# Twelve tile statistics on ScalarE, kernel rows by one-hot columns, row edits off VectorE, Toeplitz loads first, decay entries loaded inside the core

## The chip, the core and the metric

The kernel runs on one core of one Trainium2 chip. TensorE multiplies matrices, VectorE and ScalarE work on tiles, GpSimd does small elementwise work, and SyncE issues the transfers. The metric is device time in microseconds: the median of three runs of the kernel before is 955.03 us (954.43 to 955.85).

## The reference

One decoder layer on x (4 sequences of 1024 tokens, width 256) in float32. Its first part, the sequence mixer, is the one that the change touches:

```python
x = x + attn(layernorm(x))     # attn: a second layernorm, then the recurrence below, then @ W_out + b_out, with a residual
dA = exp(-exp(log_A) * dt[:, None]);  dB = B_param * dt[:, None]
h = dA * h + dB * u[..., None]                       # per channel d, 64 states n
y = einsum('dn,bdn->bd', C_param, h) + D_param * u   # for each of the 1024 steps
x = x + xattn(ctx, ctx, layernorm(x))                # 16 heads over 64 keys
x = x + ffn(layernorm(x))                            # silu(w1)*w2, two 1024x1024 gelu layers, w3
```

## The kernel before, in words

All 16 chunks of 64 steps are computed at once. For each of the 256 channels (two sets of 128, in the upper and lower half of the partitions) the recurrence becomes three products: the chunk's own output by a 64x64 lower triangular Toeplitz matrix (`within`, L477), the state that each chunk leaves (`state`, L470, with the entries `EE`, the powers of the decay), and what the carried state adds (`carried`, L484, with `GG`). Between state and carried, VectorE scans over the chunks (L431). The work on 128 channel indices goes in 16 octaves of 8, and the code for it is fully unrolled. Each octave is 48 products.

Before the core (the octaves) the following must be ready.

- `GG` is built by VectorE in six doublings (L337) from its last column. The column sums of `GG`, the kernel rows, are made by TensorE with a block of ones (L461), after D has been added to two of its one-partition rows on VectorE (L397). ScalarE evacuates them (L277), SyncE stores them to HBM (L175) and loads them back with a stride as Toeplitz matrices `ring` (L141), 16 channel indices to a group g, four groups deep. GpSimd masks each (L211). After the kernel rows, VectorE puts the two rows of `GG` back (L411).
- `EE`: SyncE loads each group of 16 with a broadcast (L146), ScalarE takes the exponential (L289).
- The tokens `tok` are normalised: VectorE's bn_stats on all 32 tiles of `xres` (L343, L346), in two batches b of 16, variances (L354), GpSimd's power (L240), spreads (L359, L363), and then 32 instructions for each batch, of which ScalarE takes 20 (`norm_apply`, L284) and VectorE 12 (`norms`, L370). VectorE multiplies by gamma and adds beta (L379, L384), in parts; three betas precede the first octave (`z_b`), the others lie between the scans.

Each engine runs its own queue in order, and semaphores order them against each other. The order is written out by hand. The groups 4 to 7 of the Toeplitz matrices are loaded inside the core, each after an octave that frees its place in the ring (`sync_core`, `w_ps`). In the core ScalarE evacuates each octave's output (L304), takes the later exponentials, and computes the residual base of 32 tiles (L292), to which GpSimd adds a bias (L216).

Of the kernel before, what the change touches and what calls it, by code (L numbers as in the profile page):

```python
# [29 lines left out]
ALU = mybir.AluOpType  # L30
# [24 lines left out]
ACT_SHARE = 20  # L55
# [3 lines left out]
def mixer_parts(nc, ctx, a, t):  # L59
# [7 lines left out]
    def sem(name):  # L67
# [12 lines left out]
    ones = sb("ones", [P, 32], "c")  # L80
# [22 lines left out]
    dtc = sb("dtc", [P, 4], "d")  # L103

    TT = [ring[:, 1024 * k:1024 * (k + 1)] for k in range(4)]
    ksb = ring[:, :].rearrange("p (a m) -> p a m", a=8)
# [7 lines left out]
    kps = [[pair[k][:, 512 * h:512 * (h + 1)] for h in range(2)] for k in (2, 0)]  # L114
# [5 lines left out]
    const, exps, coef, al_st, coef_t, pk_done, g_row, d_add = (  # L120
        sem("m_" + n) for n in ("const", "exps", "coef", "al_st", "coef_t", "pk_done", "g_row", "d_add"))
    k_ps, k_ev, kr_pad, e_rdy, t_mask = (sem("m_" + n) for n in ("k_ps", "k_ev", "kr_pad", "e_rdy", "t_mask"))
    kr_st = sem("m_kr_st")
    T_in = [sem(f"m_T_in{k}") for k in range(4)]
    stat, aggr, sv_rdy, powd, shift, spr, z_rdy, z_dve, z_h, z_b, natural, nat_v = (
# [23 lines left out]
    def sync_mixer(e):  # L149
# [16 lines left out]
        for g in range(2):  # L166
            entries_load(e, g)
        e.dma_start(bo[:, :], a["ab"].partition_broadcast(P)).then_inc(wo_in, 16)
        e.dma_start(woT[:, :, :], a["aW"]).then_inc(wo_in, 16)
        for v in range(4):  # L170
            for h in range(2):
                u = 2 * v + h
                e.wait_ge(k_ev, u + 1)
                c = (1 - h) * (P * L) + v * 2048
                e.dma_start(kr[0, c:c + 2048].rearrange("(q m) -> q m", q=4), ksb[0:P:32, u, :]).then_inc(kr_st, 16)  # L175
        for n in ("xW", "keys", "scl"):
            e.dma_start(t[n], a[n]).then_inc(k_in, 16)
# [4 lines left out]
        for g in range(2, NGRP):  # L182
            entries_load(e, g)
# [34 lines left out]
    def gpsimd_prep(e):  # L218
        e.memset(ident[:, :], 0.0).then_inc(const, 1)
        e.memset(rev[:, :], 0.0).then_inc(const, 1)  # L220
        e.memset(ones[:, :], 1.0).then_inc(const, 1)
# [4 lines left out]
        e.wait_ge(const, 6)  # L226
        e.affine_select(out=ident[:, :], in_=ident[:, :], compare_op=ALU.not_equal, fill=1.0, base=0,
                        pattern=[[-1, P]], channel_multiplier=1).then_inc(const, 1)
        for h in range(2):
            blk = rev[64 * h:64 * h + 64, 64 * h:64 * h + 64]  # L230
            e.wait_ge(const, 7 + h)
# [1258 lines left out]
```

## Time and profile before

| | us |
|---|---|
| median of three runs | 955.03 |
| the profiled execution | 954.79 |
| its span | 953.0 |
| TensorE busy | 877.2 (92%) |
| VectorE busy | 519.0 (54%) |
| ScalarE busy | 495.5 (52%) |
| GpSimd busy | 182.4 (19%) |

The span is the time from the first to the last instruction of one profiled execution. PE is TensorE, DVE is VectorE, ACT is ScalarE, POOL is GpSimd, SP is SyncE and SPq its queue of transfers. A "releaser" is what ended an engine's idle time. PEclk is the granted clock of TensorE as a share of full speed, and a DMA share of 1.00 means that all 16 engines of the core moved data all the time. In the slices of the page (one fortieth of the span, 23.8 us, each) TensorE's busy tenths begin 1, 0, 7, 9: it is nearly idle up to 48 us. The core of the mixer ends at about 102 us, the cross-attention of the first block at 155, and the loop over the other blocks fills the rest.

### The profile page before, as it was taken

What the parts mean: (1) busy time and instruction counts of PE and PEld (TensorE: products, weight loads), DVE (VectorE), ACT (ScalarE), POOL (GpSimd) and SP (SyncE); (2) the same over time, 40 slices, a digit from 0 to 9 for tenths busy, and PEclk for the clock granted to TensorE, in tenths of its full rate; (3) what the DMA queues carried; (4) which work ended last, traced back from release to release, by engine and by line L of the source; (5) the groups of instructions that cost most, each with busy time, mean ns of one, the idle gap of its engine ahead of it and who ended that gap; (6) DMA issues with size and microseconds to landing.
All of it is one profiled execution on the core that took longest, in us unless ns stands there. A gap on an engine that the chain in (4) does not pass through costs nothing.

```text
span 953.0 us, 15162 instructions
## 1 busy us (share of the span) xinstructions
PE 877.2 (92%) x5570; PEld 697.1 (73%) x5570; DVE 519.0 (54%) x927; ACT 495.5 (52%) x761; POOL 182.4 (19%) x201
## 2 busy tenths in 40 slices
PE   1079898999999999999999999999999999999996
PEld 0078876777777777777777777778778877777885
DVE  7996485555456454555555555554556465544411
ACT  2836542476356735663475536653675356636331
POOL 1567600500040003200230014000500050003000
PEclk9679999899999999999999999999999999999999
DMA  9971798500110001000200020001000110001000
GB/s 340 224 170 49 269 413 303 214 1 1 51 44 0 0 23 71 0 0 22 72 0 0 0 94 0 0 0 72 22 0 0 50 44 0 0 22 44 1 1 24
DMA packets 15784, 62.82 MB, mean 66 GB/s; under 512 B 2867, under 2 KB 4534, under 8 KB 14934
## 3 DMA queue, kind: packets, MB, share of 16 engines
q1 hardware_dynamic: 15718, 62.35, 19.2%
q8 instruction: 23, 0.38, 0.2%
q14 instruction: 11, 0.09, 0.0%
q0 software_dynamic: 32, 0.00, 0.0%
HBM read 50.16 MB, written 23.72 MB: 78 GB/s over the span
## 4 chain that ended last, share of the span: by engine, by line
PE 77%; DVE 11%; ACT 5%; issue 4%; DMA 1%; DVEq 0%; ACTq 0%; SPq 0%
PE pair L1182 47%; PE pair L1169 10%; PE pair L1118 3%; PE pair L1107 3%; PE pair L1134 3%; PE pair L539 2%; PE pair L470 2%; PE pair L1127 2%; PE pair L477 1%; PE pair L1074 1%; DVE red L932 1%; PE pair L484 1%; DVE vbuf L997 1%; DVE st L868 1%; DVE GG L337 1%
## 5 line engine op out<-in xcount | busy, mean ns | idle before, releaser
L803 ACT ACTIVATE vbuf<-pair,scl 128x512 f32<-128x512 f32 x128 | 87.8, 686 | 237.1 <-PE pair L1182 231.3
L1182 PE MATMUL pair<-h1hi,h_turned 128*128 128x512 f32 x512 | 204.0, 398 | 1.6 <-DVE h1lo L968 1.6
L1182 PE MATMUL pair<-h2hi,h_turned 128*128 128x512 f32 x512 | 202.6, 396 | 0.0
L1182 PE MATMUL pair<-h1lo,h_turned 128*128 128x512 f32 x512 | 199.8, 390 | 0.0
L1182 PE MATMUL pair<-h2lo,h_turned 128*128 128x512 f32 x512 | 199.6, 390 | 0.0
L968 DVE TENSOR_TENSOR h1lo<-vbuf,h1hi 128x512 fp32r<-128x512 f32 x80 | 57.7, 721 | 118.5 <-ACT h1hi L804 117.7
L1182 PEld LDWEIGHTS pair<-h1hi,h_turned 128*128 128x128 f32 x512 | 96.1, 188 | 34.3 <-issue 10.5
L1182 PEld LDWEIGHTS pair<-h2hi,h_turned 128*128 128x128 f32 x512 | 96.1, 188 | 25.2 <-issue 5.9
L968 DVE TENSOR_TENSOR h2lo<-vbuf,h2hi 128x512 fp32r<-128x512 f32 x64 | 44.2, 690 | 123.5 <-ACT h2hi L804 123.5
L1182 PEld LDWEIGHTS pair<-h2lo,h_turned 128*128 128x128 f32 x512 | 96.2, 188 | 19.3
L1182 PEld LDWEIGHTS pair<-h1lo,h_turned 128*128 128x128 f32 x512 | 96.2, 188 | 18.9
L1169 PE MATMUL pair<-zThi,w_turned 128*128 128x512 f32 x224 | 92.3, 412 | 5.5 <-DVE vbuf L997 5.4
L1169 PE MATMUL pair<-zTlo,w_turned 128*128 128x512 f32 x224 | 89.0, 398 | 0.0
L697 POOL TENSOR_TENSOR lnv<-lnv 128x4 f32<-128x4 f32 x16 | 16.3, 1016 | 374.6 <-DVE lnv L875 350.8
L997 DVE SCALAR_TENSOR_TENSOR vbuf<-pair,scl,sg 128x512 f32<-128x512 f32 x64 | 47.9, 749 | 66.7 <-ACT sg L792 51.2
L756 ACT ACT_TABLE_LOAD x65 | 83.4, 1283 | 1.2
L792 ACT ACTIVATE sg<-pair,scl 128x512 f32<-128x512 f32 x64 | 44.1, 689 | 65.3 <-PE pair L1169 55.0
L729 POOL TENSOR_TENSOR h1lo<-vbuf,h1hi 128x512 fp32r<-128x512 f32 x48 | 62.0, 1292 | 57.9 <-ACT h1hi L795 57.9
L470 PE MATMUL pair<-tok,EE 64*64 64x60 f32 x512 | 39.1, 278 | 24.5 <-DVE tok L384 23.2
L1169 PEld LDWEIGHTS pair<-zThi,w_turned 128*128 128x128 f32 x224 | 43.0, 192 | 22.0 <-DVE vbuf L997 11.3
L711 POOL TENSOR_TENSOR kblk<-keys,hmask 128x256 f32<-128x256 f32 x18 | 10.7, 613 | 214.7 <-PE pair L1107 214.7
L1182 PE MATMUL pair<-h1hi,w_turned 128*128 128x512 f32 x128 | 50.4, 394 | 0.0
(138 smaller groups left out, 1455.0 us busy)
## 6 DMA issues: line engine op xcount, KB each, us to landing
h_turned<-d_h SPq DMA_DIRECT2D x2, 4096.0 KB, 16.0
xres<-in_x SPq DMA_DIRECT2D x8, 512.0 KB, 7.3
tok<-in_xs SPq DMA_DIRECT2D x8, 512.0 KB, 12.2
EE<-alpha_rows SPq DMA_DIRECT2D x16, 256.0 KB, 11.6
ring<-kernel_rows SPq DMA_DIRECT2D x16, 256.0 KB, 4.4
x_rows<-x1t SPq DMA_DIRECT2D x8, 512.0 KB, 2.6
xr<-x_rows SPq DMA_DIRECT2D x8, 512.0 KB, 3.5
out<-xr SPq DMA_DIRECT2D x16, 256.0 KB, 2.1
```

What stands on the lines that cost most here:

```text
L470: ins = e.matmul(out, EE[L * h:L * h + L, i, :], rhs, start=True, stop=True)
L729: e.tensor_tensor(h1[1][:, m, :], vb[:, m % 2, :], h1[0][:, m, :], ALU.subtract).then_inc(S["lo"], 1)
L756: e.activation(warm[:, 1:2], warm[:, 0:1], function).then_inc(S["warm"], 1)
L792: e.activation(sg[:, m % 2, :], pair[m % 2][:, 0:512], ACT.Silu, scale=sc1[:, m:m + 1]).then_inc(S["sg_rdy"], 1)
L803: e.activation(vb[:, s % 2, :], h_ps[s % 4], ACT.Gelu, scale=sc)
L968: e.tensor_tensor(dst[1][:, n % HC, :], vb[:, n % 2, :], dst[0][:, n % HC, :], ALU.subtract).then_inc(S["lo"], 1)
L997: e.scalar_tensor_tensor(vb[:, m % 2, :], pair[m % 2][:, 512:1024], sc2[:, m:m + 1], sg[:, m % 2, :], ALU.mult, ALU.mult).then_inc(S["v_rd ...
L1107: ins = e.matmul(pair[2][:, g * BLK + b * 256:g * BLK + (b + 1) * 256], qa[64 * g:64 * g + 64, h, tile * P:(tile + 1) * P], kblk[64 * g:64 ...
L1118: ins = e.transpose(pair[3][:, b * BLK + r * P:b * BLK + (r + 1) * P], unit(j, u)[:, r // 2, c:c + P], ident[:, :])
L1134: ins = e.matmul(pair[3][:, m * DM:(m + 1) * DM], qa[:, k, m * P:(m + 1) * P], xwoT[:, k, :], start=(k == 0), stop=(k == DH - 1))
L1169: ins = e.matmul(pair[m % 2][:, 512 * g:512 * g + 512], w[:, k, m * P:(m + 1) * P], zT[part][:, k * BLK:(k + 1) * BLK], start=(k == 0 and ...
L1182: ins = e.matmul(bank, w[:, k, m * P:(m + 1) * P], src[part][:, k, :], start=(k == 0 and part == 0), stop=(k == HC - 1 and part == 1))
```

## The change

Five things are changed.

1. Tiles 4 to 15 of the first batch get their mean and variance on ScalarE (`tile_stats`): a Copy with an accumulated sum, two small scalings, and a Square with an accumulated sum. The elementwise outputs go to a scrap region of PSUM. VectorE keeps tiles 0 to 3 and 16 to 31. ScalarE's share of a batch's normalisations falls from 20 to 18.
2. The kernel rows are accumulated over the four groups v into one pair of banks, each group with a window of `pick` in which one column is one, so that two evacuations take the place of eight, and eight stores read four strided partitions each. ScalarE evacuates after six normalisations.
3. The copy, the addition and the restoring of the two rows of `GG` go to ScalarE and GpSimd. The clearing of two PSUM banks and of the first column of `dec` goes to the start of VectorE's program.
4. SyncE stores the kernel rows first, loads one group of entries, then the Toeplitz groups 0 to 3 alternating with entries 1 to 3, then the weights. Entries 4 to 7 are loaded inside the core, each behind the Toeplitz group of its number.
5. TensorE does three products of 512 columns into a free bank when two betas are done. VectorE does gamma and beta twice before its normalisations of the second batch. The second batch's exponentials and the residual bases come later on ScalarE, GpSimd's power over 32 columns comes behind the four masks.

```diff
-ACT_SHARE = 20
+ACT_SHARE = 18
+ACT_STATS = (4, 16)
...
-    kps = [[pair[k][:, 512 * h:512 * (h + 1)] for h in range(2)] for k in (2, 0)]
+    kps = [pair[2][:, 512 * h:512 * (h + 1)] for h in range(2)]
+    junk = [pair[0][:, DM * k:DM * (k + 1)] for k in range(4)]
...
 def sync_mixer(e):
...
+        for h in range(2):
+            e.wait_ge(k_ev, h + 1)
+            for r in range(4):
+                c = (1 - h) * (P * L) + 2048 * r
+                e.dma_start(kr[0, c:c + 2048].rearrange("(q m) -> q m", q=4), ksb[r:P:32, h, :]).then_inc(kr_st, 16)
         e.wait_ge(al_st, 32)
...
+        entries_load(e, 0)
         e.wait_ge(kr_st, 128)
         e.wait_ge(kr_pad, 16)
         for g in range(4):
             tt_load(e, g)
-        for g in range(2, NGRP):
-            entries_load(e, g)
+            if g > 0:
+                entries_load(e, g)
...
 def sync_core(e):
         for g in range(4, NGRP):
             e.wait_ge(w_ps, 2 * (g - 4) + 2)
             tt_load(e, g)
+            entries_load(e, g)
...
 def gpsimd_prep(e):
+        e.wait_ge(d_in, 32)
+        e.wait_ge(g_row, 7)
+        e.wait_ge(w_row, 2)
+        for row in (0, N):
+            v = GG[row:row + 1, :, L - 1]
+            e.tensor_tensor(v, v, edit[row:row + 1, 0, :], ALU.add).then_inc(d_add, 1)
+        e.wait_ge(d_add, 2)
+        power(0)
+        e.wait_ge(k_ps, 1)
+        e.wait_ge(powd, 1)
+        for row in (0, N):
+            e.tensor_copy(GG[row:row + 1, :, L - 1], edit[row:row + 1, 1, :]).then_inc(g_back, 1)
+        e.wait_ge(g_back, 2)
+        power(1)
+        for g in range(4):
+            mask(e, g)
...
 def scalar(e):
+        def tile_stats(first, until):
+            here, n = slice(first, until), until - ACT_STATS[0]
+            e.wait_ge(xr_in[first // 4], 16)
+            if n > 4:
+                e.wait_ge(t_var, n - 4)
+            for j in range(first, until):
+                e.activation(junk[j % 4], xres[:, j, :], ACT.Copy, accum_out=tsum[:, 0, j:j + 1]).then_inc(t_sum, 1)
+            e.wait_ge(t_sum, n)
+            e.activation(tsum[:, 1, here], tsum[:, 0, here], ACT.Copy, scale=-1.0 / (16 * DM)).then_inc(t_mean, 1)
+            e.activation(mvn[:, here, 0], tsum[:, 0, here], ACT.Copy, scale=1.0 / DM).then_inc(t_mean, 1)
+            e.wait_ge(t_mean, n // 2)
+            for j in range(first, until):
+                e.activation(junk[j % 4], xres[:, j, :], ACT.Square, bias=tsum[:, 1, j:j + 1], scale=1.0 / 16, accum_out=mvn[:, j, 1:2]).then_inc(t_var, 1)
...
+                if c == 6:
+                    row_evac()
...
 def vector(e):
-        stats(0, 4)
-        double(4)
-        stats(4, 8)
-        double(5)
...
-        stats(8, 16)
-        variances(0)
-        stats(16, 26)
+        stats(0, ACT_STATS[0])
+        last_two(0)
+        for k in range(4, 6):
+            double(k)
+        stats(SB, SB + 4)
+        variances(0)
+        stats(SB + 4, SB + 12)
         spreads(0)
-        stats(26, 32)
+        stats(SB + 12, TILES)
...
 def tensor(e):
-                    ins = e.matmul(kps[v % 2][h][32 * q:32 * q + 32, :], ones[N * h:N * h + N, 0:32], ..., start=True, stop=True)
+                    ins = e.matmul(kps[h][32 * q:32 * q + 32, :], pick[N * h:N * h + N, 3 - v:35 - v], ..., start=(v == 0), stop=(v == 3))
...
+        e.wait_ge(z_b, 2)
+        for _ in range(3):
+            e.matmul(pair[3][:, 0:BLK], ident[:, :], GGf[:, 0:BLK], start=True, stop=True)
```

SyncE's transfers ahead of the core, before (`alpha_rows` are the decay entries in HBM, `kernel_rows` the stored kernel rows; m_al_st and m_k_ev wait for the entries' store and for the evacuations):

```order
L146 DMA EE<-alpha_rows 64x1024 [waits m_al_st]
L146 DMA EE<-alpha_rows 64x1024 x3
L168 DMA bo<-in_ab 128x256
L169 DMA woT<-in_aW 128x512
L175 DMA kernel_rows<-ring 4x512 [waits m_k_ev] x8
L177 DMA xW<-in_xW 128x512
L177 DMA keys<-in_keys 128x512
L177 DMA scl<-in_scl 128x34
L141 DMA ring<-kernel_rows 64x1024 [waits m_kr_pad,m_kr_st]
L141 DMA ring<-kernel_rows 64x1024 x7
L146 DMA EE<-alpha_rows 64x1024 x12
```

And now:

```order
L173 DMA kernel_rows<-ring 4x512 x3
L150 DMA EE<-alpha_rows 64x1024 [waits m_al_st]
L150 DMA EE<-alpha_rows 64x1024
L145 DMA ring<-kernel_rows 64x1024 [waits m_kr_pad,m_kr_st]
L145 DMA ring<-kernel_rows 64x1024 x3
L150 DMA EE<-alpha_rows 64x1024 x2
L145 DMA ring<-kernel_rows 64x1024 x2
L150 DMA EE<-alpha_rows 64x1024 x2
L145 DMA ring<-kernel_rows 64x1024 x2
L150 DMA EE<-alpha_rows 64x1024 x2
L182 DMA bo<-in_ab 128x256
```

The two loads of entries (`EE`) with the Toeplitz loads (`ring`) alternate, the stores stand first, and only the groups 0 to 3 of both are left here.

SyncE's transfers inside the core, before (the last row is the first load of the feed-forward weights):

```order
L141 DMA ring<-kernel_rows 64x1024 [waits m_w_ps]
L141 DMA ring<-kernel_rows 64x1024
L141 DMA ring<-kernel_rows 64x1024 [waits m_w_ps]
L141 DMA ring<-kernel_rows 64x1024
L141 DMA ring<-kernel_rows 64x1024 [waits m_w_ps]
```

And now, the first two of four such groups:

```order
L145 DMA ring<-kernel_rows 64x1024 [waits m_w_ps]
L145 DMA ring<-kernel_rows 64x1024
L150 DMA EE<-alpha_rows 64x1024 x2
L145 DMA ring<-kernel_rows 64x1024 [waits m_w_ps]
L145 DMA ring<-kernel_rows 64x1024
L150 DMA EE<-alpha_rows 64x1024 x2
```

Behind each pair of Toeplitz loads stands a pair of loads of entries.

VectorE from the second batch's spreads on, before (`gam` and `bet` are gamma and beta, `spread` holds scale and shift):

```order
L363 COPY spread<-rn 64x2x16 [waits m_shift]
L363 COPY spread<-rn 64x2x16 x3
L411 COPY GG<-edit 1x128 [waits m_k_ps]
L411 COPY GG<-edit 1x128
L412 MEMSET dec 128x128
L379 TENSOR_TENSOR tok<-tok,gam 128x32x32 [waits m_z_dve,m_z_rdy,m_bc_in]
L370 TENSOR_SCALAR tok<-tok,spread 128x128 [waits m_x_in6,m_spr]
L370 TENSOR_SCALAR tok<-tok,spread 128x128 x3
L370 TENSOR_SCALAR tok<-tok,spread 128x128 [waits m_x_in7]
L370 TENSOR_SCALAR tok<-tok,spread 128x128 x7
L384 TENSOR_TENSOR tok<-tok,bet 128x32x32 [waits m_z_h]
L379 TENSOR_TENSOR tok<-tok,gam 128x32x32 [waits m_z_dve,m_z_rdy]
```

And now:

```order
L408 COPY spread<-rn 64x2x16 [waits m_shift]
L408 COPY spread<-rn 64x2x16 x3
L424 TENSOR_TENSOR tok<-tok,gam 128x32x32 [waits m_z_dve,m_z_rdy,m_bc_in]
L429 TENSOR_TENSOR tok<-tok,bet 128x32x32 [waits m_z_h]
L424 TENSOR_TENSOR tok<-tok,gam 128x32x32 [waits m_z_dve,m_z_rdy]
L429 TENSOR_TENSOR tok<-tok,bet 128x32x32 [waits m_z_h]
L415 TENSOR_SCALAR tok<-tok,spread 128x128 [waits m_x_in6,m_spr]
L415 TENSOR_SCALAR tok<-tok,spread 128x128 x5
L415 TENSOR_SCALAR tok<-tok,spread 128x128 [waits m_x_in7]
L415 TENSOR_SCALAR tok<-tok,spread 128x128 x7
L424 TENSOR_TENSOR tok<-tok,gam 128x32x32 [waits m_z_dve,m_z_rdy]
L429 TENSOR_TENSOR tok<-tok,bet 128x32x32 [waits m_z_h]
```

The two copies into `GG` and the clearing of `dec` are gone; two gammas and two betas now precede the 14 normalisations of the second batch, where one gamma preceded 12.

## Rows read from the trace of the kernel before

**Rows 1.** Chain of waits up to 84 us: start, length, what.
```profile
28.66 3.63 ACT tok L284 x10
...
37.47 1.23 DVE tok L379
...
49.53 1.86 PE pair L470 x30
...
55.20 3.20 issue
...
70.45 1.61 issue
...
83.41 1.27 issue
```

**Rows 2.** DMA view, instruction queue, windows 55.4:56, 69:70 and 84:98: packets, MB, share.
```profile
q8 instruction: 1, 0.02, 13.5%
...
q8 instruction: 1, 0.02, 6.9%
...
q8 instruction: 4, 0.07, 1.9%
```

**Rows 3.** Time line of SyncE from 64 to 70 us: start, length, what.
```profile
65.67 1.09 SPq L141 DMA_DIRECT2D ring<-kernel_rows  x2
```

**Rows 4.** Windows view: length, each engine busy (instructions), PEclk, DMA share, GB/s.
```profile
52.00:54.00 2.00, 2.00 (x80) 2.00 (x74) 2.00 (x5) 0.00 (x0) 1.80 (x3) 0.50 1.04 229
64.00:66.00 2.00, 2.00 (x84) 2.00 (x78) 2.00 (x4) 0.05 (x1) 1.31 (x2) 1.00 0.04 8
66.50:69.50 3.00, 2.90 (x110) 2.80 (x107) 3.00 (x8) 2.67 (x6) 1.36 (x1) 1.00 0.71 175
```

**Rows 5.** Time line of VectorE: start, length, instruction, idle time before it.
```profile
6.04 0.58 DVE L332 COPY edit<-pair 1x128 f32<-1x128 f32 x2
...
14.87 4.40 DVE L337 TENSOR_TENSOR GG<-GG,pk 128x4096 f32<-128x4096 f32 x1
19.40 0.84 DVE L397 TENSOR_TENSOR GG<-GG,edit 1x128 f32<-1x128 f32 x2
...
26.81 0.40 DVE L343 BATCH_NORM_STATS2 stn<-xres 128x6 f32<-128x256 f32 x1
...
27.20 0.40 DVE L343 BATCH_NORM_STATS2 stn<-xres 128x6 f32<-128x256 f32 x1
...
27.77 0.80 DVE L363 COPY spread<-rn 64x32 f32<-64x32 f32 x4
```

**Rows 6.** Time line of GpSimd, power and first mask.
```profile
23.96 2.93 POOL L240 TENSOR_TENSOR rn<-sv,mhalf 128x16 f32<-128x16 f32 x1 [20.06 <-DVE sv L354]
...
40.30 2.42 POOL L211 TENSOR_SCALAR_AFFINE_SELECT ring<-ring 64x1024 f32<-64x1024 f32 x2 [5.90 <-DMA ring<-kernel_rows]
```

**Rows 7.** Time line of ScalarE.
```profile
3.47 0.20 ACT L264 ACTIVATE dtc<-dtc 128x2 f32<-128x2 f32 x1 [1.37 <-DMA dtc<-in_log_dt]
...
5.99 0.95 ACT L269 ACTIVATE pk<-pair 128x128 f32<-128x128 f32 x5
...
22.44 1.08 ACT L277 ACTIVATE ring<-pair 128x512 f32<-128x512 f32 x2 [13.50 <-PE pair L461]
...
28.66 7.81 ACT L284 ACTIVATE tok<-tok,spread 128x128 f32<-128x128 f32 x20 [1.09 <-issue]
...
67.49 1.08 ACT L292 ACTIVATE xres<-xres,ngn,rsn 128x256 f32<-128x256 f32 x2
```

**Rows 8.** Windows view, VectorE on tile tok alone: length, busy (instructions), PEclk, DMA.
```profile
32.50:35.50 3.00, 2.96 (x12) 0.50 0.43 144
...
40.00:42.00 2.00, 2.00 (x4) 0.50 1.04 236
```

**Rows 9.** Time line of SyncE, first Toeplitz loads.
```profile
35.45 4.96 SPq L141 DMA_DIRECT2D ring<-kernel_rows  x8
```

**Rows 10.** Chain of waits at 199 us, 512-column products.
```profile
198.90 3.66 PE pair L1182 x16
```

More of the change, by code:

```diff
@@ L79, in mixer_parts @@
     rev = sb("rev", [P, P], "c")
-    ones = sb("ones", [P, 32], "c")
+    pick = sb("pick", [P, 35], "c")
     stn = sb("stn", [P, TILES, 6], "d")
@@ L220, in gpsimd_prep @@
         e.memset(rev[:, :], 0.0).then_inc(const, 1)
-        e.memset(ones[:, :], 1.0).then_inc(const, 1)
+        e.memset(pick[:, :], 0.0).then_inc(const, 1)
         e.memset(mhalf[:, :], -0.5).then_inc(const, 1)
@@ L230, in gpsimd_prep, with power @@
             blk = rev[64 * h:64 * h + 64, 64 * h:64 * h + 64]
-            e.wait_ge(const, 7 + h)
+            e.wait_ge(const, 8 + h)
             e.affine_select(out=blk, in_=blk, compare_op=ALU.not_equal, fill=1.0, base=-63,
                             pattern=[[1, 64]], channel_multiplier=1).then_inc(const, 1)
-        e.wait_ge(const, 9)
+        e.wait_ge(const, 10)
         e.dma_start(kr[:, DM * L:DM * L + L], rev[0:1, L:2 * L]).then_inc(kr_pad, 16)
-        for b in range(2):
+        def power(b):
             here = slice(SB * b, SB * b + SB)
@@ L245, in gpsimd_prep @@
         e.wait_ge(natural, 1)
-        for g in range(1, 4):
-            mask(e, g)
-        e.wait_ge(t_mask, 8)
     def gpsimd_core(e):
@@ L292, in residual_base @@
             e.activation(xres[:, j, :], xres[:, j, :], ACT.Identity, bias=ngn[:, j:j + 1], scale=rsn[:, j:j + 1]).then_inc(base, 1)
-        for v in range(4):
-            row_evac(v)
-        e.wait_ge(const, 9)
+        for first in range(*ACT_STATS, 4):
+            tile_stats(first, first + 4)
+        e.wait_ge(const, 10)
         norm_apply(0)
-        entry_exp(0)
         norm_apply(1)
-        for g in range(1, 3):
+        for g in range(3):
             entry_exp(g)
@@ L304, in scalar @@
             e.activation(tok[:, :, OCT * o:OCT * o + OCT], yps[o % 4].rearrange("p (i c) -> p c i", i=OCT), ACT.Copy).then_inc(y_out, 1)
-            if o % 2 == 0 and 3 + o // 2 < NGRP:
+            if o % 2 == 1 and 3 + o // 2 < NGRP:
                 entry_exp(3 + o // 2)
-            if o == 2:
+            if o == 5:
                 e.wait_ge(natural, 3)
-            until = 0 if o < 2 else min(2 * o - 2 + max(0, o - 8), TILES)
+            until = 0 if o < 5 else min(3 * (o - 4), TILES)
             for j in range(done, until):
@@ L321, in vector @@
     def vector(e):
+        for k in range(2):
+            e.memset(hps[k], 0.0).then_inc(h_zero, 1)
+        e.memset(dec[:, :, 0], 0.0).then_inc(dec0, 1)
         e.wait_ge(exps, 2)
@@ L330, in vector @@
         e.tensor_copy(GG[:, :, L - 1:L], wT.unsqueeze(2)).then_inc(g_row, 1)
-        for row in (0, N):
-            e.tensor_copy(edit[row:row + 1, 1, :], wT[row:row + 1, :]).then_inc(d_add, 1)
         def double(k):
@@ L343, in stats, with last_two @@
                 e.bn_stats(stn[:, j, :], xres[:, j, :]).then_inc(stat, 1)
+                n = j if j < SB else j - (ACT_STATS[1] - ACT_STATS[0])
                 if j % SB >= 2:
-                    e.wait_ge(stat, j - 1)
+                    e.wait_ge(stat, n - 1)
                     e.bn_aggr(mvn[:, j - 2, :], stn[:, j - 2, :]).then_inc(aggr, 1)
+        def last_two(b):
+            until, n = (ACT_STATS[0], TILES)[b], ACT_STATS[0] + SB * b
+            for j in (until - 2, until - 1):
+                e.wait_ge(stat, n - (until - 1 - j))
+                e.bn_aggr(mvn[:, j, :], stn[:, j, :]).then_inc(aggr, 1)
         def variances(b):
-            for j in (SB * b + SB - 2, SB * b + SB - 1):
-                e.wait_ge(stat, j + 1)
-                e.bn_aggr(mvn[:, j, :], stn[:, j, :]).then_inc(aggr, 1)
-            e.wait_ge(aggr, SB * b + SB)
+            n = ACT_STATS[0] + SB * b
+            if b == 0:
+                e.wait_ge(t_var, ACT_STATS[1] - ACT_STATS[0])
+            e.wait_ge(aggr, n)
             here = slice(SB * b, SB * b + SB)
@@ L418, in vector @@
         beta(1)
+        norms(1)
         gamma(2)
```

68 lines of the change are left out of this document (27 added, 41 removed).

## The prediction

> **What bounds the kernel now.** I read the busy table and the slices first: over the 953.0 us TensorE is busy 92%, and the slices in which it is not are the first three, about 70 us. The change ends before the cross-attention, so I read only the stretch up to 105 us, in the chain of waits. The reader sees there [rows 1]: ScalarE's twenty normalisations (20 instructions from 28.66, two pieces of ten), a gamma product at 37.47, then VectorE's own normalisations with more gamma and beta, and TensorE's first state product at 49.53. Behind it the chain has three stretches called issue: 3.20 us at 55.20, 1.61 at 70.45, 1.27 at 83.41. No engine is waited for in them. What ends them is seen only in the DMA view: a queue named instruction brings single packets of 0.02 MB, and one lies at 55.4 to 56, one at 69 to 70 [rows 2], each some 2.5 to 3 us before TensorE goes on. From 84 to 98, with nothing else to load, four come in 14 us [rows 2], one each 3.5 us. So TensorE's unrolled code is streamed, and it runs little ahead. A packet that is late is lost time. At 65.67 two Toeplitz loads are issued [rows 3]; the DMA engines are 71% busy from 66.5 to 69.5 [rows 4], the packet comes behind them, and TensorE stands 1.61 us.
>
> The clock reads 0.50 from 52 to 54 and 1.00 from 64 to 66 (1.2 and 2.4 GHz), but these small products pass at 80 and 84 per 2 us [rows 4]: 5%.
>
> **The change, part by part.**
>
> *Up to the first spreads.* Gone from VectorE before the doublings: two row copies (0.58 us at 6.04 [rows 5]); with an overlap of 0.2 the doublings begin 0.4 earlier. The last doubling (4.40 us, [rows 5]) now stands behind 4 statistics instead of 8. A statistic with its aggregation costs 0.39 (two starts are 26.81 and 27.20 [rows 5]), so the last doubling ends at about 19.3 - 0.4 - 4 x 0.39 = 17.3 us. The two row edits (0.84 [rows 5]) go to GpSimd; one-partition adds on GpSimd aren't in the trace, I take 1.0 (between nothing and the 2.93 of its 16-element power [rows 6]). The kernel rows start at 18.5 instead of 20.4, which buys nothing: they are evacuated only after six normalisations on ScalarE.
>
> ScalarE's statistics begin when the decay broadcast and two row copies are done, about 9.4. One pass over 128x256 with no pointer lies between the 128x128 copies (five in 0.95, 0.17 apart) and the 128x512 ones (two in 1.08): 0.31. With two pointers it is 0.49 apart (two in 1.08), with one, like the squares, I take 0.40 [rows 7]. A group of four tiles is 4 x 0.31 + 4 x 0.40 + two tiny scalings and three waits on its own results, together 0.75: 3.6 us. The accumulator output isn't in the trace. At least it is free; as a tiny instruction of its own (0.20 us [rows 7], 0.11 apart) it adds 8 x 0.11 = 0.9; at 0.3 each it adds 2.4. I take 0.9, so three groups take 13.5 us and end at 22.9 (20.2 to 27.4).
>
> VectorE waits for it: it has only four more statistics in front (to 18.9). Power on GpSimd 2.93 [rows 6], with eight statistics beside it, then one shift and four copies (0.80 [rows 5]), 1.0: the first spreads are ready at about 27.1, against 28.6 (27.77 + 0.80 [rows 5]). Call this moment A. It is 1.5 us earlier (24.4 to 31.6 by the two ends). Twelve statistics off VectorE would be 4.7 us; most of it becomes a wait for ScalarE.
>
> *From A to the core.* ScalarE: 18 normalisations at 0.39 (twenty take 7.81 [rows 7]) and the two evacuations (1.08) are 8.1, before 7.8. VectorE then does gamma, beta, gamma, beta (1.14 to 1.25 each, after [rows 1]), 4.8: A + 13.0. Only now its 14 normalisations. Alone each takes 0.24 (12 in 2.96 us); while GpSimd masks, four in 2.00 [rows 8]. The masks start when the first Toeplitz load lands. The evacuated rows are ready at A + 3.0 to A + 3.5. Eight stores follow, 0.5 us each (two issues take 1.09 [rows 3]), then some 2 us until the last has landed (my estimate for 8 KB on quiet engines). The first Toeplitz load is issued at A + 8.9 (before at 35.45 [rows 9], which was A + 6.9). From issue to mask it took 4.85 us before (40.30 [rows 6]); the mask starts at A + 13.7, before at A + 11.7. So masks 0 and 1 (2.42 us a pair [rows 6]) lie on the normalisations: four of the 14 at 1.2, ten at 0.24, 7.2 us. With gamma and beta 2.4 more the core starts at A + 22.6 = 49.7, against 49.53. If the masks missed them it were 3.8 earlier. ScalarE's first decay exponential is ready at A + 16.4, the first mask at A + 16.2: hidden. The three dummy matmuls sit in A + 13 to A + 22.6; by the 0.23 us in which a 512-column pass runs at the full clock (16 in 3.66 [rows 10]), 3 x 4 passes at half of it are 5.5 us, hidden too. They give the first products the full clock perhaps; by the 5% above that is 0.3 us.
>
> *Code and loads.* The first packet is asked for shortly into the core. Before, it came between 55.4 and 56 [rows 2], behind full engines (busy share 1.04 at 52 to 54 [rows 4]), and TensorE went on at 58.40 [rows 1]. Now 1.5 MB of entries less (three groups behind the first, not six) stand in the queue together with the Toeplitz rows (at 229 GB/s [rows 4] 14 load instructions of 0.26 MB are 16 us from A + 10): they end at about A + 26 = 53, and 1.1 MB of weights and biases at 56. A packet asked for at 50.5 then passes when the entries are through, at 53.7, and TensorE goes on 2.7 later, at 56.4: 2.0 us earlier than 58.40. The packet after it is no longer held by that queue, for which I take 0.4 more: 2.4 earlier.
>
> But groups 4 to 7 of the entries now go out behind the Toeplitz loads inside the core: four instructions and 1 MB each time instead of 0.5. The engines are full for about 5 us instead of 2.7 (from 66.5 on at 175 GB/s over 3 us [rows 4]). Code packets come every 3.5 us and these loads every two octaves, about 5.4 us: a window of 2.7 catches some (two clear stalls, 1.61 and 1.27 [rows 1]; I allow 0.4 for smaller ones), a window of 5 catches nearly all. Counting on from the restart with one packet each 3.5 us and a load pair each two octaves, four of seven packets fall into a window, each held back 1.6 (as at 70.45) to 2.1 us (a load that lasts longer): 4 x 1.8 = 7.3, against 3.3. That is +4.0. SyncE's queue has nothing urgent behind these loads. Group 4's exponential is needed only three octaves on: hidden.
>
> Sum on the profiled execution: -2.4 + 4.0 = +1.6 on 953.0. Behind the core nothing changes: ScalarE still has three residual tiles in front of its last two evacuations; its two last tiles come behind them, in the time in which TensorE turns the first block. GpSimd's 32-element power moves behind the four masks and is wanted by VectorE at octave 4, some 5 us after it is ready. The profiled run took 954.79, 1.79 over its span and 0.24 under the median of 955.03; I add the 1.6 to the median: **956.6 us**.
>
> **The rivals.** *The code is not held back (952.6).* If a packet gets in between the loads, the +4.0 vanishes and -2.4 stays. For it: four Toeplitz pairs are loaded inside the core, and only two of them show a stretch of over 1 us. Against it: the stalls at 70.45 and 83.41 stand exactly where loads and packet met, with only 0.5 MB loaded. The Trainium skill, "Runtime: NRT & Kernel Launch", section "Instruction fetch mechanics", says that the sequencer fetches the next page while it executes the current one, and that the cost of a boundary is mostly hidden. By that rule this rival would be the forecast. The trace disagrees in this stage, with 3.20, 1.61 and 1.27 us.
>
> *ScalarE's statistics are dear (959.6).* The point is the wait of the first variances for the last of the twelve. If an accumulating pass costs 0.3 more, it ends at 27.4 and A at 31.6, 3.0 later than before; the core starts 4.5 later than I put it, part of which the emptier queue gives back, so I price it at +3 over my sum. It decides from the point at which a group of four takes more than 5.0 us (then A is where it was). For it: VectorE has nothing to do but wait from 18.9. Against it: the nearest rows are cheap.
>
> *The start is early (954).* The accumulator is free and A at 24.4, or the masks miss the normalisations. The start gains 3 us, but the first packet is held longer in a fuller queue, and the +4.0 stays: about -1 in all.
>
> **Chances.** Forecast 45%, code not held 25%, dear statistics 20%, early start 10%. The forecast's own range is 954.5 to 958.5 (windows that catch three or five packets, 1.8 us each). To hold 8 in 10 it must take in most of both rivals: 952 to 960. A measurement of this kernel tells 0.2%, 1.9 us. Faster by more: most of the second case and a little of the last, 24%. Slower by more: the dear case and two fifths of the forecast, 36%. Within: 40%.
>
> **What would show it.** Right: VectorE idle several us before its first variances, the spreads near 27, the first state product near 50, the first issue stretch ended near 56.4, and then about four stretches of issue over 1 us from 60 to 87 us, each with a code packet at the end of a Toeplitz and entries load. Wrong: issue stretches that are gone or no longer than before (then the first rival), or ScalarE's twelve statistics past 25 us (the second). What would make the total wrong with every step right is the phase: how the packets fall against the loads is a matter of some tenths of a us.

## The result

| | before | after |
|---|---|---|
| median, us | 954.58 (951.36 to 955.85, 6 runs) | 958.36 (956.86 to 961.93, 6 runs) |
| profiled execution, us | 954.79 | 958.09 |
| its span | 953.0 | 956.4 |
| TensorE busy | 877.2 | 880.7 |

The ratio is 1.0051, interval [1.0026, 1.0075]: slower by more than the 0.2% that can be told from no change. The forecast was 956.6, and its range of 952 to 960 holds the time. TensorE's busy time grows by 3.5 us, but that isn't the cause: the three dummy products alone take 4.4 us (from 40.4 to 44.9), and TensorE waits anyway until 51.

The profile after. The chain of waits (start, length, what), which answers to [rows 1]:

```profile
22.49 4.81 issue
27.30 2.42 ACT tok L321 x6
...
40.18 7.45 DVE tok L415 x14
...
48.98 2.05 DVE tok L429
...
51.07 1.86 PE pair L507 x30
...
56.21 2.38 issue
...
66.36 1.34 issue
...
71.31 2.28 issue
...
81.55 1.41 issue
...
86.59 1.70 issue
```

L415 is VectorE's fourteen normalisations of the second batch, L429 its beta, L507 the first state product. Four issue stretches of 1.34 to 2.28 us follow the first one, where before had two (1.61 and 1.27). The DMA view has one packet of the instruction queue in each of 65 to 66, 70.5 to 71.5, 80 to 81 and 85 to 86 us; TensorE goes on at 67.7, 73.6, 83.0 and 88.3, each time 2.4 to 2.9 us behind its packet. SyncE begins to issue the four groups of loads at 59.7, 65.5, 74.8 and 80.8, 4.7 to 5.6 us ahead of these packets.

Time line of ScalarE, a part of the first group of four statistics, and the end of the last (to [rows 7]):

```profile
10.67 0.37 ACT L301 ACTIVATE pair<-xres 128x256 f32<-128x256 f32 x1
10.97 0.19 ACT L301 ACTIVATION_READ_ACCUMULATOR pair<-xres 128x1 f32 x1
11.07 0.36 ACT L301 ACTIVATE pair<-xres 128x256 f32<-128x256 f32 x1
...
12.93 0.46 ACT L307 ACTIVATE pair<-xres,tsum 128x256 f32<-128x256 f32 x1
13.32 0.19 ACT L307 ACTIVATION_READ_ACCUMULATOR pair<-xres,tsum 128x1 f32 x1
13.42 0.46 ACT L307 ACTIVATE pair<-xres,tsum 128x256 f32<-128x256 f32 x1
...
22.30 0.19 ACT L307 ACTIVATION_READ_ACCUMULATOR pair<-xres,tsum 128x1 f32 x1
```

An accumulated sum is a second instruction of 0.19 us. Passes follow each other every 0.40 (sums) and 0.49 us (squares).

Time line of VectorE and then of GpSimd (to [rows 5, 6, 8]); brackets hold the idle time before:

```profile
22.52 0.18 DVE L399 TENSOR_SCALAR sv<-mvn 128x16 f32<-128x16 f32 x1 [3.36 <-ACT pair L307]
...
26.02 1.20 DVE L408 COPY spread<-rn 64x32 f32<-64x32 f32 x4
...
29.27 3.67 DVE L415 TENSOR_SCALAR tok<-tok,spread 128x128 f32<-128x128 f32 x14
...
40.18 7.43 DVE L415 TENSOR_SCALAR tok<-tok,spread 128x128 f32<-128x128 f32 x14
```

```profile
17.86 1.14 POOL L251 TENSOR_TENSOR GG<-GG,edit 1x128 f32<-1x128 f32 x2 [13.80 <-DVE GG L375]
...
41.47 5.05 POOL L214 TENSOR_SCALAR_AFFINE_SELECT ring<-ring 64x1024 f32<-64x1024 f32 x4 [9.10 <-DMA ring<-kernel_rows]
```

The same number of normalisations, fourteen, take 3.67 us at 29.27 and 7.43 at 40.18, when GpSimd's masks run beside them. The time line taken instruction by instruction shows how: beside the four masks (5.05 us, 1.26 each) four of the fourteen take 1.24 to 1.31 us each, the others about 0.26. This is the 4 x 1.2 and 10 x 0.24 of the prediction.

Time line of SyncE (to [rows 3, 9]), and the DMA view's instruction queue from 55.8 to 56.4 us (to [rows 2]):

```profile
35.74 2.44 SPq L145 DMA_DIRECT2D ring<-kernel_rows  x4
...
65.50 1.22 SPq L145 DMA_DIRECT2D ring<-kernel_rows  x2
66.76 1.24 SPq L150 DMA_DIRECT2D EE<-alpha_rows  x2
```

```profile
q8 instruction: 1, 0.02, 11.3%
```

The windows view, columns as in [rows 4]. First 48 to 56 us of after:

```profile
48.00:52.00 4.00, 0.93 (x18) 0.93 (x20) 3.96 (x3) 1.15 (x1) 3.63 (x2) 0.50 1.03 228
52.00:54.00 2.00, 2.00 (x66) 2.00 (x66) 2.00 (x4) 0.00 (x0) 1.16 (x2) 0.52 1.02 221
54.00:56.00 2.00, 2.00 (x79) 1.98 (x74) 2.00 (x3) 0.00 (x0) 1.85 (x3) 1.00 1.06 340
```

The first packet comes at 56.0 to 56.1. The DMA engines are full until then and for 1 us longer. From 54 on they move 340 GB/s instead of 221: the entries are through, and what moves are the weights and biases.

Then the measure for the rest of this document: the window from the restart behind the first code packet over some 765 products of the core. Its length less TensorE's busy time is what TensorE lost there. Before, and under it after:

```profile
58.40:84.70 26.30, 23.00 (x767) 21.90 (x767) 21.12 (x41) 14.81 (x24) 14.41 (x19) 0.94 0.41 102
```

```profile
58.60:88.30 29.70, 22.62 (x765) 21.77 (x766) 20.57 (x42) 13.05 (x21) 18.97 (x21) 0.94 0.56 145
```

Before loses 3.30 us there, after 7.08. That is +3.8. The window is 3.4 us longer (TensorE is busy 0.4 less in it), and so is the span: nearly the whole result lies in these 30 us.

### The profile page after: what moved, and what is told of

It reads as the page before. It is cut to its first block, busy times and chain, and to the rows that moved or that the text cites. A ratio compares the mean times of both kernels' runs of the same rounds, so it can differ in the third digit from the quotient of the medians.

```text
span 956.4 us, 15206 instructions
## 1 busy us (share of the span) xinstructions
PE 880.7 (92%) x5576; PEld 698.2 (73%) x5576; DVE 515.4 (54%) x901; ACT 503.4 (53%) x807; POOL 184.0 (19%) x206
## 4 chain that ended last, share of the span: by engine, by line
PE 77%; DVE 9%; ACT 5%; issue 5%; DMA 1%; DVEq 0%; ACTq 0%; SPq 0%
PE pair L1219 47%; PE pair L1206 10%; PE pair L1155 3%; PE pair L1144 3%; PE pair L1171 3%; PE pair L507 2%; PE pair L576 2%; PE pair L1164 2%; PE pair L1111 1%; PE pair L514 1%; DVE red L969 1%; PE pair L521 1%; DVE vbuf L1034 1%; DVE st L905 1%; DVE red L984 1%
## 5 line engine op out<-in xcount | busy, mean ns | idle before, releaser
L1219 PE MATMUL pair<-h1hi,w_turned 128*128 128x512 f32 x128 | 50.4, 394 | 0.0
L507 PE MATMUL pair<-tok,EE 64*64 64x60 f32 x512 | 39.6, 277 | 11.4 <-DVE tok L429 6.2
```

The source lines that it names most:

```text
L507: ins = e.matmul(out, EE[L * h:L * h + L, i, :], rhs, start=True, stop=True)
L1219: ins = e.matmul(bank, w[:, k, m * P:(m + 1) * P], src[part][:, k, :], start=(k == 0 and part == 0), stop=(k == HC - 1 and part == 1))
```

## The experiments

Ratios are to the kernel before, run beside each on the same chip, five rounds each. The theory: TensorE's code comes in packets, one for each 256 matmul and weight-load instructions; a packet that is asked for while data fill the DMA engines is late, and TensorE stands for it. Times within a kernel are of one profiled execution each, and the ratios of the timed runs decide.

**e1: before, with idle bytes.** Two entry loads that nothing uses behind each of the four Toeplitz pairs in the core.

```diff
+            for h in range(2):
+                e.dma_start(EE[L * h:L * h + L, GRP * (g - 4):GRP * (g - 3), :].rearrange("p d n -> p (d n)"),
+                            bass.AP(t["alS_h"], (8 * h + g - 4) * (GRP * N), [[0, L], [1, GRP * N]])).then_inc(again, 16)
```

> The kernel before, with one thing added: inside the core each Toeplitz pair (groups 4 to 7) is followed by two loads of 0.26 MB that read the raw decay entries of a group already used once more into its own place, which nobody reads. Theory (code packets of TensorE stand behind data on the DMA engines): four load windows of about 5 us instead of 2.7, so issue stretches grow by 3 to 4 us in all between 60 and 88 us and the median rises by 3.5 us (ratio about 1.0037), with the same start of the core (49.5) and the same first restart (58.4). Rival (the changed kernel is late because ScalarE's exponentials or GpSimd's masks come late and hold the products): nobody waits for these loads, so nothing changes (ratio 1.000).

Measured: 958.62, ratio 1.0043 [1.0028, 1.0058]. The windows view, the same products:

```profile
59.90:88.70 28.80, 22.16 (x767) 21.05 (x766) 20.15 (x39) 14.79 (x24) 14.29 (x13) 1.00 0.56 150
```

6.64 us are lost, 3.3 more than before. No instruction of the core waits for these bytes, so as many bytes as the change adds bring nearly its whole loss (3.3 of 3.8) without a late exponential or mask. One part of the expectation missed: with nothing changed ahead of the core, its first product starts at 51.3 here and not at 49.5, and TensorE goes on at 59.9 and not at 58.4.

**e2: before, with entries 4 to 7 in the core** as the change has them.

```diff
-        for g in range(2, NGRP):
+        for g in range(2, 4):
             entries_load(e, g)
...
             tt_load(e, g)
+            entries_load(e, g)
```

> The kernel before, with the entries of groups 4 to 7 loaded inside the core, each behind its Toeplitz pair, and nothing else changed. Theory: the core starts at 49.5 as before, the queue ahead of it is 1 MB x 2 shorter (about 9 us of loads) and is through at about 51, so the first issue stretch ends near 55 instead of 58.4 (-3.4); the four windows in the core then cost +3.5. Sum about 0 (ratio 0.998 to 1.002). Rival (only the loads inside the core matter, the first stretch has another cause than the queue): first stretch stays, ratio 1.0037.

Measured: 953.70, ratio 0.9997 [0.9985, 1.0008]. The core starts at 50.4, and the queue runs empty as it does (DMA share 0.61 from 50 to 51, 0.00 from 51 to 52). The first packet (instruction queue, 51.8 to 52.4 us) comes 1.7 us behind the start, where before it was 5.9; the windows view follows:

```profile
q8 instruction: 1, 0.02, 9.6%
```

```profile
52.00:54.00 2.00, 2.00 (x76) 2.00 (x76) 1.97 (x6) 0.00 (x0) 1.93 (x2) 0.50 0.03 8
55.80:82.10 26.30, 22.12 (x773) 21.14 (x766) 23.79 (x46) 14.85 (x24) 16.53 (x21) 0.99 0.63 164
```

TensorE passes the first page at 55.8 without a stop, where before did at 58.4. The same loads inside the core cost 4.18 us here, 0.9 more than before, not the 3.3 of e1. In this execution the gain that the prediction put on the start exists, with an empty queue, and the price of the loads depends on how they fall. But it is the fastest of the kernel's twelve runs (951.01, the median is 953.70), and the timed ratio shows no gain in the sum.

**e3: the changed kernel, with entries 4 to 7 ahead of the core** (behind the Toeplitz groups; the edit of e2 turned round).

```diff
+        for g in range(4, NGRP):
+            entries_load(e, g)
...
             tt_load(e, g)
-            entries_load(e, g)
```

> The changed kernel with the entries of groups 4 to 7 ahead of the core again, behind the other loads of entries and ahead of the weights. Theory: the four long issue stretches between 60 and 88 us go back to two of 1 to 2 us, but the queue is full until about 62, so the first restart is near 59.3 and the second packet is held too; +1.5 us against the kernel before, 2 us faster than the changed kernel (ratio 1.0015). Rival (the later start of the core is the whole loss): still 1.005.

Measured: 959.22, ratio 1.0053 [1.0040, 1.0067]: missed. The chain shows why:

```profile
55.41 3.23 issue
...
63.04 3.71 issue
```

The first stretch is 3.23 us and the second, 3.71, is new. The 2 MB moved ahead keep the engines full beyond 64 (DMA share 1.06 from 62 to 64), and the second packet is late too; it lies at 64 to 65. Of the stretches behind it three of 1.01, 0.74 and 1.45 us are left. The loss has moved towards the start of the core.

**e4: the changed kernel, with all statistics on VectorE.**

```diff
-        for first in range(*ACT_STATS, 4):
-            tile_stats(first, first + 4)
...
-        stats(0, ACT_STATS[0])
+        stats(0, 4)
...
+        stats(4, 16)
+        last_two(0)
```

> The changed kernel with all 32 statistics on VectorE again (ScalarE's share of the normalisations stays 18). Theory: VectorE's idle 3.4 us before the first variances vanish and the variances come at the same 22.5 us; the first spreads come 1.3 us later because twelve and not eight statistics lie behind the power; the total is 1 us above the changed kernel (ratio against before about 1.0062). Rival (ScalarE's statistics are what costs): faster than the changed kernel by 1 us or more.

Measured: 959.80, ratio 1.0048 [1.0035, 1.0061], against 1.0051 of the changed kernel: neither the 1 us more that was expected nor the rival's 1 us less. VectorE's time line has the spreads 0.85 us later:

```profile
27.27 0.80 DVE L404 COPY spread<-rn 64x32 f32<-64x32 f32 x4
```

Yet the first state product starts at 50.9 against 51.07: VectorE's last beta takes 1.22 us here and 2.04 beside a mask in the changed kernel, the normalisations 7.25 and 7.43, and this takes the 0.85 back. The twelve statistics on ScalarE neither gain nor cost anything that can be measured.

**e5: the changed kernel, with the second batch's normalisations directly behind their spreads,** before gamma and beta and so before the masks.

```diff
+        norms(1)
...
-        norms(1)
```

> The changed kernel with VectorE's 14 normalisations of the second batch directly behind the second spreads (33.9 us), ahead of gamma and beta and of the masks. Theory: alone they take 3.4 us instead of 7.4 and fill the 1.5 us in which VectorE waited for ScalarE, so the core starts near 45 to 46 instead of 51.1; but the queue is full then, the first packet is held for the full 4.5 us and the second until the weights are through (56), so only about 4 us reach the end: ratio against before about 1.001 (after: 1.0051). Rival (the start of the core decides alone): 5.5 us or more, ratio 0.999 or less. Rival (the code queue decides alone and the start nothing): ratio stays 1.005.

Measured: 955.75, ratio 1.0009 [1.0000, 1.0018]. VectorE's time line, and the chain:

```profile
33.77 3.68 DVE L415 TENSOR_SCALAR tok<-tok,spread 128x128 f32<-128x128 f32 x14
```

```profile
47.17 1.70 PE pair L507 x30
...
52.15 2.76 issue
```

3.68 in place of 7.43, the core starts 3.9 earlier and goes on at 54.9 instead of 58.6. This is worth 0.4%, as was expected. The 3.9 us are not the masks' effect alone: the 1.52 us in which VectorE waited are filled too, some gammas and betas now lie beside masks instead (2.17 and 2.05 us at 42.15 and 44.35), and at the end the core waits for the dummy products until 47.1.

One more thing is seen here. SyncE issues the same loads at the same times as in the changed kernel (to 0.2 us), and the entries are through at the same time (the rate rises in 54 to 55 in both). The first packet comes at 52.2, in the middle of the entries, and not at 56.0. It lies 5.1 us behind the core's start, in the changed kernel 5.0. So the packet goes with TensorE's program there, not with the end of the entries or of the weights.

**e6: e5, with entries 0 to 3 loaded ahead of the stores of the kernel rows,** when the queue is idle.

```diff
+        e.wait_ge(al_st, 32)
+        for g in range(4):
+            entries_load(e, g)
         for h in range(2):
             e.wait_ge(k_ev, h + 1)
...
-        e.wait_ge(al_st, 32)
-        entries_load(e, 0)
...
-            if g > 0:
-                entries_load(e, g)
```

> The kernel of e5 with the entries of groups 0 to 3 moved ahead of the stores of the kernel rows, into the time from about 24 to 34 us in which the DMA engines of the changed kernel are idle; groups 4 to 7 stay inside the core. Theory: Toeplitz loads and weights are through by about 49, the first packet is held 3 us at most, the second not at all; the first restart is near 52 (after: 58.6), the four long stretches in the core stay. Ratio against before about 0.9965. Rival (the queue ahead of the core doesn't matter once the start is early): same as e5.

Measured: 953.38, ratio 0.9981 [0.9972, 0.9991], a gain of 0.3% on e5 where 0.45% was expected. TensorE passes the first packet without a stretch of over 0.3 us, but loses 6.4 in the rest.

**e7: e6, with entries 0 to 5 early, 6 and 7 behind the Toeplitz groups, none in the core.**

```diff
-        for g in range(4):
+        for g in range(6):
...
+        for g in range(6, NGRP):
+            entries_load(e, g)
...
-            entries_load(e, g)
```

> The kernel of e6 with groups 0 to 5 ahead of the stores and 6 and 7 behind the Toeplitz loads, none inside the core. Theory: two stalls of 1 to 2 us remain in the core instead of four, which gives back about 3.5 us, but the queue is full until 56 again and holds the first two packets (restart near 54.6, second boundary near 59), which costs about the same: ratio 0.9965, between 0.995 and 0.999. Rival (only the loads inside the core cost): 3.5 us faster than e6.

Measured: 953.76, ratio 0.9985 [0.9975, 0.9994], inside its range but no better than e6. The chain:

```profile
55.47 3.95 issue
...
63.96 1.77 issue
...
81.72 1.45 issue
```

The first packet lies at 48.3, only 1.6 us behind the start of the core at 46.7, with the engines full, and TensorE doesn't stand for it; for the second, at 56.7 with the engines as full, it stood 3.95 us. How long a full queue holds a packet isn't settled by its being full.

**e8: e6, without the three products of 512 columns ahead of the core.**

```diff
-        e.wait_ge(pk_done, 7)
-        e.wait_ge(w_row, 2)
-        e.wait_ge(z_b, 2)
-        for _ in range(3):
-            e.matmul(pair[3][:, 0:BLK], ident[:, :], GGf[:, 0:BLK], start=True, stop=True)
```

> The kernel of e6 without the three products of 512 columns that TensorE does into a free bank before the core. Theory: the small products pass at nearly the same pace at either clock and the first blocks of code wait for their packets anyway: within 0.5 us of e6, and the clock reads 0.50 in the first products instead of 1.00. Rival (the warming is worth its place): 1 us or more slower than e6.

Measured: 952.88, ratio 0.9977 [0.9968, 0.9986], as e6. TensorE's time line of e6 has the dummy products in its way; that of e8 starts the core 2.2 us earlier:

```profile
42.38 5.42 PE L498 MATMUL pair<-GG,ident 128*128 128x512 f32 x6 [17.38 <-DVE tok L428]
47.73 1.76 PE L506 MATMUL pair<-tok,EE 64*64 64x60 f32 x30
```

```profile
45.55 1.86 PE L501 MATMUL pair<-tok,EE 64*64 64x60 f32 x30 [20.65 <-DVE tok L428]
```

The packets lie at 50.5 (e6) and 50.7 (e8), and TensorE goes on behind both at 53.1: the packet bounds it there, and not the start of the core. Why the two packets lie together, 2.8 and 5.1 us behind their starts, isn't shown; the engines are full at that time in both. And the clock (0.50 in e8 from 46 to 50, 1.00 in e6 from 48 to 52) decides nothing here.

**e9: before, with the Toeplitz pairs issued at chosen products.** SyncE waits for TensorE to pass a fixed product, chosen just behind the point where a packet has been asked for.

```diff
-        for g in range(4, NGRP):
-            e.wait_ge(w_ps, 2 * (g - 4) + 2)
-            tt_load(e, g)
+        for n, (toeplitz, entries) in enumerate((((4,), ()), ((5,), ()), ((6,), ()), ((7,), ()))):
+            e.wait_ge(pace, n + 1)
+            for g in toeplitz:
+                tt_load(e, g)
...
+                    if (o, c) in ((3, 0), (4, 3), (7, 0), (8, 3)):
+                        ins.then_inc(pace, 1)
```

> The kernel before, with one edit: the four Toeplitz pairs of groups 4 to 7 are not issued as soon as their buffer is free, but when TensorE reaches a fixed product of the core, chosen to fall just behind the point at which a code packet has been asked for (one every 256 recorded instructions). Nothing is computed differently. Theory (a code packet that stands behind data in the queues is held, and the hold is lost 1:1): the two issue stretches of rows 1 at 70.45 (1.61) and 83.41 (1.27) go, 2.5 to 3 us less, ratio 0.997. Rival (bytes brought in during the core decide, whenever they are asked for): no change, ratio 1.000. Rival with the other sign (the Toeplitz pairs now arrive late): a wait for the load at the first product of a group, 1 us and more, ratio above 1.001.

Measured: 953.21, ratio 0.9983 [0.9974, 0.9992].

```profile
58.80:81.80 23.00, 22.66 (x766) 21.77 (x765) 19.49 (x42) 14.80 (x24) 8.98 (x12) 0.93 0.33 97
```

The window loses 0.34 us in place of 3.30. The same four pairs are loaded, and no wait for them comes up in it. Timed, the gain is 1.6 us, not the 2.5 to 3 expected. Behind this window 256 instructions take 3.9 to 4.1 us (before 3.6) with the DMA engines idle (share 0.02): from 85.7 to 97.7 TensorE is busy for 10.94 of 12.00 us, standing 0.3 to 0.4 at the end of each page. That gives a part of the 3.0 back; why it does is open.

**e10: the changed kernel, with all eight loads in the core so placed.** Order: entries 4, Toeplitz 4, 5, entries 5, Toeplitz 6, then Toeplitz 7 with entries 6, then entries 7.

```diff
+        for n, (toeplitz, entries) in enumerate((((), (4,)), ((4,), ()), ((5,), ()), ((), (5,)), ((6,), ()), ((7,), (6,)), ((), (7,)))):
+            e.wait_ge(pace, n + 1)
...
+                    if (o, c) in ((1, 5), (3, 0), (4, 3), (5, 5), (7, 0), (8, 3), (9, 5)):
+                        ins.then_inc(pace, 1)
```

> The changed kernel, with one edit: the four Toeplitz pairs and four entry loads inside the core are issued one or two at a time when TensorE reaches fixed products, each just behind the point at which a code packet has been asked for. Theory of held packets: of the four long issue stretches of the changed kernel inside the core (1.34, 2.28, 1.41, 1.70) at most one stays (two loads share one point), 5 us less than the changed kernel, ratio to before 1.000 (0.998 to 1.002). Rival (the bytes inside the core decide, not their moment): ratio stays 1.005.

Measured: 953.75, ratio 0.9984 [0.9971, 0.9997], 0.7% under the changed kernel and inside its range of 0.998 to 1.002. Windows, then the chain behind it:

```profile
58.20:81.00 22.80, 22.39 (x768) 21.71 (x770) 19.96 (x42) 10.73 (x17) 12.50 (x15) 0.93 0.45 134
```

```profile
80.59 6.45 DMA EE<-alpha_rows
```

0.41 us lost in place of 7.08. The core starts no earlier than in the changed kernel (the restart is at 58.2, there at 58.6). The entries issued last, now late, become a wait of their own: between 84.7 and 88.3 TensorE stands for some 3 us, and a part of the gain is left there.

**e11: e8, so paced, with entries 6 early too.**

```diff
-        for g in range(4):
+        for g in (0, 1, 2, 3, 6):
             entries_load(e, g)
```

> The kernel of e8 with the paced loads of e10, and the entries of group 6 ahead of the core as well, so that no point carries two loads. Theory of held packets: three of e8's four stretches in the core go, 4 to 6 us less than e8 (952.88), ratio to before 0.992 to 0.994. Rival (moment does not matter): as e8, 0.998.

Measured: 947.57, ratio 0.9914 [0.9901, 0.9928], a little under the 0.992 to 0.994 expected; e8 had 0.9977. It beats both kernels, the one before by 0.9%.

```profile
53.10:76.00 22.90, 21.34 (x761) 20.74 (x762) 20.30 (x42) 11.40 (x18) 19.21 (x17) 1.00 0.48 134
```

1.56 us are lost there; e8 loses 6.34 over the same products.

**e12: e9 at the wrong moment,** 1.75 us later, and nothing else changed.

```diff
-                    if (o, c) in ((3, 0), (4, 3), (7, 0), (8, 3)):
+                    if (o, c) in ((3, 5), (5, 0), (7, 5), (9, 0)):
```

> The kernel of e9, in which the same four Toeplitz pairs are issued at four other products, 1.75 us later, so that a pair is on its way when the next code packet is asked for. Number, size and spacing of the loads are those of e9, and each group still lands 11 us and more before its first product. Theory (the hold of a code packet behind data decides): each of four packets starts 1 to 2 us later than in e9, four issue stretches of about 1 to 1.5 us come back, 3 to 5 us more than e9 (953.21), ratio to before 1.001 to 1.004. Rival (it is the spacing of the loads that helped in e9, not their moment): as e9, 0.998.

Measured: 955.80, ratio 0.9991 [0.9982, 1.0000].

```profile
59.60:84.20 24.60, 22.44 (x764) 21.61 (x763) 19.51 (x39) 14.77 (x24) 8.00 (x8) 0.93 0.27 71
```

2.16 us lost against 0.34 in e9: the direction is that of the theory, the size about half of what was expected. The expected ratio of 1.001 to 1.004 was missed. In time the difference to e9 is 0.08%, and the two intervals overlap, so by the timed runs alone moment and spacing aren't told apart.

## Why the prediction was right or wrong

*Up to the first spreads: right.* ScalarE's statistics were put to end at 22.9; they end at 22.49. A was put at 27.1; the spreads are out at 27.22. The accumulator read is the 0.1 us apart that the prediction took. The two row edits on GpSimd cost 1.14 for 1.0.

*From A to the core: right in its kind, 1.4 us short.* VectorE begins the fourteen normalisations at 40.18 (put at A + 13.0 = 40.1, with the wait for ScalarE's eighteen in it), the mask is at 41.47 (put at 40.8), the normalisations take 7.4 (7.2), and the core starts at 51.07 (49.7). Up to here it is right to some tenths; what was missed is a last beta of 2.04 us beside a mask, put at 1.2, and some tenths around it. The same happens by chance in the kernel before: e1, e9 and e12 have its program ahead of the core unchanged, and their first products start at 51.30, 50.23 and 51.26, against 49.53 in its own profile. VectorE's last gamma or beta beside a mask, 2.04 to 2.16 us instead of 1.2, is the difference. So the 1.4 us are no more than executions of one program differ by. The dummy products (L499, 4.44 us from 40.41) are hidden, as forecast.

In e5 the fourteen normalisations without masks take 3.75 us less, near the 3.8 of the prediction.

*The start gain of 2.4: wrong.* This is the term that failed. The packet was to pass at 53.7, when the entries are through, and TensorE to go on at 56.4. The packet lies at 56.0, 2 us into the weights, and TensorE goes on at 58.6, 0.2 later than in the profile before. The 2.5 us from packet to restart are near the forecast (2.7). What failed is the step that ties the packet to the end of the entries. The entries are through at about 54 (put at 53), and the packet doesn't come with them; in e5, with the same queue, it comes before that, at 52.2. In both it lies 5.0 to 5.1 us behind the core's start, before 5.9, and 1.7 in e2 with the queue empty. So an emptier but still full queue brought 0.9 us in these two profiles, and the later start of the core took them. By the other executions the gain is no larger: with the start of the kernel before TensorE goes on at 58.4, 59.9, 58.8 and 59.6 (before, e1, e9, e12), with that of the changed kernel at 58.6 and 58.2 (after, e10), 0.8 earlier in the mean. What sets the packet's time in a full queue stays open: e7 has it 1.6 us behind the core's start.

*Code and loads, +4.0: right.* 7.3 against 3.3 was forecast for the stalls behind the restart (its 4 x 1.8 is 7.2); 7.08 against 3.30 is what the two windows lose. Four stretches of over 1 us stand there, each with a packet, as forecast. That the sizes agree so well is in part luck: the prediction itself calls the phase of packets and loads a matter of tenths, and e2, with the same loads in the core, loses 4.18. e1 shows the same with bytes that no one uses, e9 and e10 that nearly all of it goes (0.34 and 0.41 left) with the same loads issued at other moments. The rule beside which the prediction set a rival, the Trainium skill's "Runtime: NRT & Kernel Launch", "Instruction fetch mechanics" (the next page is fetched during the current one, the boundary is mostly hidden), agrees with e9's window, where the loads are out of the way and the loss is 0.34 us over six packets. It doesn't agree with the windows before and after, nor quite with e9 behind its window (1.06 us in 12.00, engines idle).

*Why the hold varies: open.* In e7 the first packet is hardly held and the second for some 4 us, both behind full engines. The Trainium skill's "DMA: Bandwidth & Descriptors", section "Queues, rings and completion order", says under Arbitration that an engine takes turns between its queues a packet at a time, and drains a whole packet first; by that a single code packet would wait for one data packet on its engine and not for a queue. e3 and e7, with 3.2 to 4 us of standstill behind full engines, don't look like this, but no run here shows the engine's ring itself. Whether the spacing of the loads or their moment did the more in e10 is open too: e12 gives the moment 1.8 us of 3.0 in the profile, and no difference that the timed runs can confirm.

The sum was -2.4 + 4.0 = +1.6. In the profile it is +0.2 for the restart and +3.8 of more loss, less 0.4 in which TensorE is busy less: +3.6 at 88 us, of which the rest gives 0.2 back: +3.4. Timed it is 0.51%, 4.9 us (2.5 to 7.2 by the interval). So the sum was short by the start gain, and that the time still lies in the range is owed to the range, which was drawn wide to take in both rivals. ScalarE's statistics, which the title of the change names first, had no part in it that can be measured (e4).

## What to carry to other kernels

Where the chain of waits says issue on TensorE and the program is unrolled small products, look for the instruction queue in the DMA view: code is streamed, and loads in the core compete with it. Count the loss as window length less busy time over the same products. Then change when the loads go out, not only their bytes: place each just behind a code request, one at a time (e9, e10, e11; which of the two does more isn't shown). A load moved ahead helps where the queue is idle: entries put there gave 0.3% (e6 against e5), entries put behind a full queue gave nothing (e3 against the changed kernel). And compare profiles with care: the start of this core differs by 1.8 us between executions of the same program.

## What the runs showed of the hardware

- One code packet for each 256 matmul and weight-load instructions of the core; in e9's window six take 23.0 us, 3.8 each, and TensorE is busy for 22.66 of it. Behind it, with the DMA engines idle, TensorE still stands 0.3 to 0.4 us a page: streaming runs level with these small products, with next to no reserve. TensorE goes on 2.4 to 3.0 us behind a packet for which it stood (72.1 for the packet in 69 to 70 and 58.4 for that in 55.4 to 56, before).
- An accumulated output on ScalarE is an own instruction of 0.19 us, 0.10 apart.
- VectorE's normalisations of 128x128 take 0.26 us each alone; of those beside GpSimd's masks each takes as long as a mask, 1.24 to 1.31 us (3.67 and 7.43 us for fourteen, four of them beside masks). A gamma or beta of 128x1024 takes 1.2 alone and 2.04 to 2.17 beside a mask.
- Small products run nearly as fast at half the clock: in e8 80 of them pass in 48 to 50 us at 0.50, before 84 in 2 us at 1.00 [rows 4].
